# The norms' weight products move from the ternary layer into the channel attention; batch statistics one per slot

## What is computed

```python
x = x + tanh(g_xattn[0]) * L0_xattn(layernorm(x), ctx, mask, mask, ...)   # attention over channels, 16 heads of 8
x = x + tanh(g_ffn[0])   * L0_ffn(layernorm(x), ...)                      # ternary weights, 8-bit activations
x = x + tanh(g_xattn[1]) * L1_xattn(layernorm(x), ctx, ...)               # token attention, rms norm of q and k
x = x + tanh(g_ffn[1])   * L1_ffn(layernorm(x), ...)                      # attention and routed experts

q = rms_norm(x @ q_w + q_b, nq_s)     # in L1_xattn: the mean square goes over all 16 heads x 128
k = rms_norm(ctx @ ki_w + ki_b, nki_s)
```

## Time and profile before

| | |
|---|---|
| Three executions | 1869.86, 1876.90, 1881.18 us; median 1876.9 us |
| The profiled execution | span 1872.4 us, 34349 instructions |
| TensorE busy | 1729.6 us (92%) |
| VectorE busy | 1150.4 us (61%) |
| ScalarE busy | 976.9 us (52%) |
| GpSimd busy | 519.3 us (28%) |
| Mean granted clock of TensorE | 0.952 of 2.4 GHz |

### The profile page before, as it was taken

The page is one execution under the profiler, slowest core; times in us unless marked ns, Lnnn a source line. Parts: engine busy times, 40 slices in busy tenths (PEclk is TensorE's granted clock), DMA queues, the critical chain, the costliest instruction groups (busy, mean ns, idle before and its releaser), DMA issues. The chain is left out here.

```text
span 1872.4 us, 34349 instructions
## 1 busy us (share of the span) xinstructions
PE 1729.6 (92%) x11722; PEld 1454.1 (78%) x11722; DVE 1150.4 (61%) x2612; ACT 976.9 (52%) x2534; POOL 519.3 (28%) x570
## 2 busy tenths in 40 slices
PE   7999996897699999999999999999999988698887
PEld 6666663655588888888888888888888886587775
DVE  6689983897655656556566655555555658633334
ACT  2588875586354545545555545454454437344442
POOL 4133321253411111111122111121111221656663
PEclk7799996998899999999999999999999989899998
DMA  4111121202100100100100021001000024423346
GB/s 151 59 36 36 37 82 35 109 9 94 49 13 1 46 12 12 35 12 12 35 24 23 12 61 35 12 12 35 1 12 1 1 74 123 136 78 112 97 132 223
DMA packets 48914, 97.38 MB, mean 52 GB/s; under 512 B 7466, under 2 KB 29146, under 8 KB 47764
## 3 DMA queue, kind: packets, MB, share of 16 engines
q1 hardware_dynamic: 40023, 72.44, 12.7%
q0 software_dynamic: 7584, 21.37, 3.8%
q10 hardware_dynamic: 1144, 1.40, 0.2%
HBM read 73.85 MB, written 20.97 MB: 51 GB/s over the span
## 5 line engine op out<-in xcount | busy, mean ns | idle before, releaser
L2050 POOL TENSOR_TENSOR hold_wq<-hold_wq,ca_rsum 128x512 f32<-128x512 f32 x128 | 133.5, 1043 | 811.0 <-DVE ca_rsum L2290 811.0
L1906 ACT ACTIVATE hold_wq<-hold_wq,ca_nb,ca_evens 128x128 f32<-128x128 f32 x256 | 123.4, 483 | 226.9 <-DVE ca_nb L2285 226.9
L1906 ACT ACTIVATE hold_wq<-hold_wq,ca_nb,c_rqs 128x128 f32<-128x128 f32 x256 | 123.4, 483 | 223.8 <-DVE ca_nb L2285 223.8
L712 DVE TENSOR_REDUCE a_mx<-a_s 128x2 f32<-128x512 f32 x256 | 164.9, 681 | 43.3 <-PE a_s L584 40.6
L503 ACT ACTIVATE a_prob<-a_s 128x512 f32<-128x512 f32 x256 | 146.7, 604 | 61.1 <-PE a_s L604 60.0
L2066 PE MATMUL ca_qk<-early_x,ca_wqkv_h 128*128 128x512 f32 x384 | 161.5, 421 | 11.3 <-DVE ca_wqkv_l L2235 11.3
L2068 PE MATMUL ca_qk<-early_x,ca_wqkv_l 128*128 128x512 f32 x384 | 152.3, 397 | 0.0
L2067 PE MATMUL ca_qk<-early_x,ca_wqkv_h 128*128 128x512 f32 x384 | 151.6, 395 | 0.0
L2187 PE MATMUL ca_acc<-ca_wo_h,ca_oT_h 128*128 128x256 f32 x512 | 145.1, 283 | 0.2 <-DVE ca_oT_l L2299 0.2
L2189 PE MATMUL ca_acc<-ca_wo_h,ca_oT_l 128*128 128x256 f32 x512 | 144.4, 282 | 0.0
L2188 PE MATMUL ca_acc<-ca_wo_l,ca_oT_h 128*128 128x256 f32 x512 | 144.4, 282 | 0.0
(11 more groups left out here) (496 smaller groups left out, 4903.8 us busy)
## 6 DMA issues: line engine op xcount, KB each, us to landing
early_big<-slot_results SPq DMA_DIRECT2D x16, 512.0 KB, 4.7
mw_raw<-in_d_expert_w SPq DMA_DIRECT2D x12, 352.0 KB, 5.6
a_heads<-a_osb SPq DMA_DIRECT2D x124, 32.0 KB
a_wraw<-a_heads SPq DMA_DIRECT2D x31, 128.0 KB, 2.1
mw_down<-in_d_expert_d SPq DMA_DIRECT2D x1, 2816.0 KB
token_rows<-early_rows SPq DMA_DIRECT2D x1, 2176.0 KB
hold_wk<-in_c_wkT SPq DMA_DIRECT2D x1, 2064.0 KB
hold_wq<-in_c_wqT SPq DMA_DIRECT2D x1, 2064.0 KB
```

Source lines behind the costliest of these rows:

```text
L712: dve.tensor_reduce(mx[:, b % 2, :, h], s1_bank(b, u)[:, :, :], AX.X, ALU.max)\
L1906: ins = act.activation(prob[:, p, b, :], prob[:, p, b, :], ACT.Exp, bias=nb[:, p, b:b + 1], scale=row_scale[layer][:, r:r + 1], accum_out= ...
L2050: pool.tensor_tensor(prob[:, k % 2, :, :], prob[:, k % 2, :, :], rsum[:, k % 2, :].unsqueeze(2).broadcast_to([P, GB, TOKENS]), ALU.mult)\
```

## The change

`KeyWork` gets the three steps of a product (`multiply` for one head, `keep_high`, `keep_low`), and the channel attention runs them: product 0 in slots 0 to 10 and product 1 in slots 13 to 23, one or two heads a slot, both in the bank `out`; product 2 in slots 239 to 254, one head a slot, in `proj[0]`; product 3 behind the last slot, in a score bank. The evictions stand in the slot behind each product, the last ones at the end of ScalarE's and VectorE's queues. TensorE waits for a lower half before it writes the bank again. The ternary layer loses all of this. The fetch of the key weights goes ahead of the three transfers of 1536 KB, that of the query weights from behind batch 11 to behind batch 10. The measures of batches 4 to 15 go from threes in the slots below 0 to one a slot in slots 4 to 15, `condense` to slot 17, the power to 21, the bias to 26.

```diff
+    def multiply(self, pe, i, h, bank):
+
+        n, k = divmod(i, KT)
+        if h == 0:
+            pe.wait_ge(self.ld_w[n], 16)
+        mm = pe.matmul(bank[:, 0:GW], self.weights[n][:, h, P * k:P * k + P], self.weights[n][:, h, :],
+                       start=(h == 0), stop=(h == HEADS - 1))
+        if h == HEADS - 1:
+            mm.then_inc(self.gram_psum, 1)
+
+    def keep_high(self, act, i, bank):
+        act.wait_ge(self.gram_psum, i + 1)
+        act.activation(self.high(i // KT, i % KT), bank[:, 0:GW], ACT.Copy).then_inc(self.gram_hi, 1)
+
+    def keep_low(self, dve, i, bank):
+        dve.wait_ge(self.gram_hi, i + 1)
+        dve.tensor_tensor(self.low(i // KT, i % KT), bank[:, 0:GW], self.high(i // KT, i % KT).bitcast(F32),
+                          ALU.subtract).then_inc(self.gram_lo, 1)
...
 
+        gram_bank = [b[:, :, :].rearrange("p a n -> p (a n)") for b in (out, out, proj[0], s1[0])]
+
...
-        REST_POW, REST_BIAS = 12, 20
+        MEASURED, CONDENSED = 4, 17
+        REST_POW, REST_BIAS = 21, 26
+        GRAM_FROM, GRAM_SLOTS = (0, 13, 239), (11, 11, 16)
+
+        def gram_of(t):
+
+            for i, (a, n) in enumerate(zip(GRAM_FROM, GRAM_SLOTS)):
+                if 0 <= t - a < n:
+                    return i, range(HEADS * (t - a) // n, HEADS * (t - a + 1) // n)
+            return 0, range(0)
+
+        def gram_made(t):
+
+            return {a + n: i for i, (a, n) in enumerate(zip(GRAM_FROM, GRAM_SLOTS))}.get(t)
         ORDER = ("q0", "q1", "k0", "k1", "v0")
...
                                  mparts[BATCHES * k:BATCHES * k + BATCHES, :].bitcast(F32)).then_inc(m_ext, 16)
+                work.fetch(sp, 0)
                 sp.dma_start(x_sb[:, rest, :], io["x"][rest].rearrange("b p n -> p b n")).then_inc(ld_x[1], 16)
                 sp.dma_start(ctx_sb[:, rest, :], io["ctx"][rest].rearrange("b p n -> p b n")).then_inc(ld_c[1], 16)
...
                 maxima(1)
-                work.fetch(sp, 0)
                 for b in range(BATCHES):
                     gather(b)
                     if b + 2 < BATCHES:
                         maxima(b + 2)
-                    if b == 11:
+                    if b == 10:
                         sp.wait_ge(cm_ready, BATCHES)
                         work.fetch(sp, 1)
...
                         if copied(t)[1] == 0:
                             gated_mask(copied(t)[0])
                         copy_out(*copied(t))
+                    if gram_made(t) is not None:
+                        work.keep_high(act, gram_made(t), gram_bank[gram_made(t)])
...
                 act.wait_ge(x_done, 3 * (BATCHES - 2))
                 act.dma_start(den[:, p, :], heads[p, 1]).then_inc(moved[p], 16)
+                work.keep_high(act, 3, gram_bank[3])
...
                     o = out_bank(b, j // 2)
                     if j == 0:
                         pe.wait_ge(v_ready, b + 1)
+                    if b == 0 and j == 0:
+                        pe.wait_ge(work.gram_lo, 2)
+                    if j % 2 == 0 and o is proj[0]:
+                        pe.wait_ge(work.gram_lo, 3)
                     if j % 2 == 0 and o is not out:
                         pe.wait_ge(k_stack, 2 * BATCHES)
                         pe.wait_ge(v_ready, BATCHES)
...
+
+                def gram_room(i):
+                    if i == 1:
+                        pe.wait_ge(work.gram_lo, 1)
+                    if i == 2:
+                        pe.wait_ge(k_stack, 2 * BATCHES)
+                    if i == 3:
+                        pe.wait_ge(prob_ready, ALL)
...
                             project(b, *PIECES[u], 1)
                         if u == 13:
                             project_v(b)
+                    i, turns = gram_of(t)
+                    for h in turns:
+                        if h == 0:
+                            gram_room(i)
+                        work.multiply(pe, i, h, gram_bank[i])
+                gram_room(3)
+                for h in range(HEADS):
+                    work.multiply(pe, 3, h, gram_bank[3])
...
                     u, b = t % U, built(t)
                     if b is not None and u in (2, 6, 10, 14):
                         stack_piece(b, *PIECES[u - 2])
-                    if t < 0 and u % 4 == 2:
-                        n = FIRST + 3 * (u // 4)
-                        dve.wait_ge(ld_x[1], 16)
-                        measure(n, n + 3)
-                    if t == 0:
+                    if FIRST <= t - MEASURED + FIRST < BATCHES:
+                        n = t - MEASURED + FIRST
+                        if n == FIRST:
+                            dve.wait_ge(ld_x[1], 16)
+                        measure(n, n + 1)
+                    if t == CONDENSED:
                         condense(FIRST, BATCHES, 2 * FIRST)
                     if t == REST_BIAS:
                         mean_bias(FIRST, BATCHES, 1)
...
                         invert(closed(t), 1)
                         if closed(t) == BATCHES - 1:
                             close_last()
+                    if gram_made(t) is not None:
+                        work.keep_low(dve, gram_made(t), gram_bank[gram_made(t)])
+                work.keep_low(dve, 3, gram_bank[3])
...
@@ -860,7 +920,6 @@
-                sp.wait_ge(gram_psum, 4)
...
                 turned_scale(0)
-                gram_high(0)
                 scaled_weights(0)
...
                     if n == 0:
                         pe.wait_ge(weights_ready, w + 1)
-                        if w == 1:
-                            pe.wait_ge(gram_lo, 3)
...
                 def turn_h(n):
                     after(pe, hT_ready, n)
-                    if n == 0:
-                        pe.wait_ge(gram_lo, 4)
...
-                gram(0, 0)
-                gram(0, 1)
                 weight_sum(0)
-                gram(1, 0)
                 turn_scale(0)
                 weight_sum(1)
...
-                    if n == -1:
-                        gram(3, 0)
...
-                        gram(1, 1)
-                        gram(2, 0)
-                        gram(2, 1)
                     if n == -1:
                         turn_scale(1)
-                        gram(3, 1)
...
                     for n in range(a, b):
-                        if n == 10:
-                            gram_low(2)
...
                     if n == -1:
                         clip_weights(2)
-                        gram_low(3)
```

28 lines of the change are left out of this document (1 added, 27 removed).

## The result

The changed kernel took 1882.11 us (median of 20 runs, 1877.47 to 1885.54), the kernel before 1874.44 us beside it (20 runs): a ratio of **1.0034** [1.0024, 1.0043], or 6 to 8 us slower. Beside other kernels on another chip it was 1.0033 [1.0020, 1.0046]. I had forecast 2 us faster. The size is within the half per cent that I had called hard to tell, but twenty runs tell it, and it has the other sign. The profiled execution has a span of 1882.1 us.

A forecast was written before the change was run, and what follows sets the result against it. Opening bound by VectorE, then half-clock TensorE; closing also lost clock; ternary prologue waited on VectorE's chain, then ScalarE. Opening +0.4, closing -1.3, end +0.45, ternary -1.5 made -2.0 us: 1875 us from median 1876.9, range 1864 to 1883.

The forecast's parts named there:

- Opening, slots 0 to 23: Channel attention's opening: TensorE's added heads and lone score slots at 0.43 us make slot 24 8.4 us later.
- The first rival: Opening and closing: a lone score slot costs 0.22 us, not 0.43; 1865 us in all, chance 0.17.
- Opening, slots 24 to 34: Behind both opening products: TensorE without gaps keeps clock 1.00, 7.6 us less; whole opening +0.4 us.
- the second rival: Clock falls in slots 24 to 30, VectorE bounding, and in the last batch: opening +7, 1888 us, chance 0.10.
- Measures and fetch: Opening: one-per-slot measures and early weight fetch cost 0; measures gone from before slot 0 give 0.4 us less.
- Closing: Slots 239 to 254 and behind: slot 258 1.1 us later, ScalarE and last weighing faster at full clock; -1.3 us.
- End: Behind the last slot: product 3 hidden under the closing chain, its low half behind VectorE's last addition; +0.45 us.
- Ternary layer: Its prologue: without products and evictions the scale rows come 1.9 us earlier, low clock gives 0.4 back; -1.5 us.
- Sum: Whole kernel: opening, closing, end and ternary terms together -2.0 us, giving 1875 us.

The follow-up runs named there:

- e11: Changed kernel with products 0 and 1 in groups of two or three heads, mostly in even slots 0 to 26 and slot 27; ratio 0.9984 to the kernel before.
- e8: The changed kernel run again with no edit; ratio 1.0033 to the kernel before.
- e13: Kernel before with only the measures, condensing and early weight fetch moved, all products left in the ternary layer; ratio 1.0013.
- e17: Kernel before with the measures moved as in the change, products and weight fetch as before; ratio 1.0012.
- e2: Kernel before with only products 2 and 3 moved to the channel attention, single heads in slots 239 to 254; ratio 1.0020.
- after: The changed kernel in its first profile; 1882.11 us, ratio 1.0034 to the kernel before.
- e7: Changed kernel plus 64 unneeded multiplies in the ternary layer where the products stood before, without evictions; ratio 1.0034 to the kernel before.
- e10: Changed kernel with product 1 in slots 17 to 27 instead of 13 to 23; ratio 1.0040 to the kernel before.
- e4: Changed kernel with products 0 and 1 in groups of five and six heads, product 2 in pairs in even slots; ratio 1.0024 to the kernel before.
- e15: Changed kernel with products 0 and 1 in groups of two and three, product 2 in pairs, product 3 back in the ternary layer; ratio 0.9978 to the kernel before.
- e12: Changed kernel with products 0 and 1 in groups of two and three heads and product 2 in pairs in even slots; ratio 0.9968 to the kernel before.
- e5: Kernel before with only products 2 and 3 moved, product 2 as two heads in each even slot 240 to 254; ratio 1.0013.
- e3: Kernel before with only product 3 moved, behind the last slot of the channel attention; ratio 1.0006.
- e6: Changed kernel plus six unneeded multiplies, two in each of slots 256 to 258; ratio 1.0040 to the kernel before.
- e9: The kernel before run again with no edit; ratio 0.9994.

## Why the prediction was wrong, point by point

**Opening, slots 0 to 23: right.** I had 8.4 us more at slot 24 from 21 lone slots at 0.43; measured 8.1 and 7.7. The first rival (a lone slot is cheap) is out. The rule that I had weighed from the Trainium skill (TensorEngine Tiling (Array Packing), "Key Properties": a change of tiling mode drains the engine) agrees with it: with half the changes (e11) some 5 us of the 8.1 vanish.

**Opening, slots 24 to 34: the step that failed.** I had 7.6 us back, since TensorE would have no gap and the clock 1.00: 10.3 us from slot 24 to slot 34's piece. They took 11.6 in the first profile and 14.5 to 15.5 in the four others. TensorE was full at 1.00 from 28 to 64 us, but then came two waits for ScalarE's first exponentials, 1.08 us together, which I had not looked for: I checked VectorE as the second bound there, in the second rival, and not the first exponentials. Slot 34 was at +1.8 in the first profile and +3.8 to +4.7 in the four others with this opening, slot 238 at +0.7 and +2.9 to +4.1. Term: +0.4 forecast, some **+3** measured. The second rival had the mechanism, but with +7 us and a clock that does not come back; it was back after 7 to 10 us. That rival was to turn on TensorE's share in these slots, which I had at 90%; it was 2.92 of 4 us, in the profile that kept the clock as in e8, which lost it.

**Measures and fetch: 0 and -0.4 us forecast.** Slot 0 came 0.1 to 1.2 us earlier, right. The 2 us that e13 and e17 measured I did not have; where they arise is open (above).

**Closing: -1.3 forecast.** Three sizes were off. A slot without a weighing took 1.06 us and a fourth of the slots, with one, 2.06: 1.31 us a slot on average where I had 1.2 (the head costs 0.63 and not 0.47 when it stands alone), and slot 258 came 3.5 us later than slot 238's piece would have it, not 1.1. From slot 242's turned maxima to slot 255's scores the rows above give 0.32 + 4 x 1.0 (weighings) + 13 x 0.63 + 12 x 0.43 = 17.7 us; I had 15.6, with thirteen quarters of a weighing where four whole ones stand and no turned maxima. The last three slots took 2.4 us and not 1.7, with 0.98 of waiting for exponentials. And the clock fell at 302 us, behind the last head, so that ScalarE's gain of 2.3 us came in full, of the kernels with lone heads, only in e2 (2.6 us from slot 258 to the last weighing; e8 1.3, after 0.2). From slot 238 to the last addition, kernels with lone heads took 0.7 to 3.4 us more than before (after 2.9, e8 1.8, e2 0.7, e7 3.4, e10 3.1, e11 2.4), with pairs -2.1 to +1.0 (e4, e15, e12, e5), and with no product there -3.9 to +1.5. Lone heads cost some **+2.5**, pairs about nothing; device times say the same of the step from one to the other (e11, e12).

**End: +0.45 forecast, +0.1 measured.** Product 3 took 7.25 us (319.35 to 326.6) under the closing chain, as forecast. Its low half stands behind the last addition, but from that addition to the next layer's first instruction were 1.85 us instead of 1.73: the meeting of all engines covers it. e3 measures 1.0006 [0.9989, 1.0023].

**Ternary layer: -1.5 forecast.** The seven kernels that take all products out of it (after, e4, e6, e8, e10, e11, e12) took -1.1 to +0.1 us from its first instruction to its last addition against the first profile of before, -0.7 in the mean; the second profile of before took +1.3. The saving is about 1 us and comes with products 0 and 1: the second scale rows begin 41.3 to 42.7 us after the layer's first instruction in the seven profiles without added work that keep these two there (before, e2, e3, e5, e9, e13, e17) and 39.9 to 40.9 in the twelve that don't, wherever products 2 and 3 stand. The 1.1 us that I had for the last product's own place is not there (e3, which moves this product alone: 41.8). The scale rows came 40.7 us after the layer's first instruction, not 38 as the prediction wrote nor the 39.7 of its own sum (41.6 before).

**Sum.** Some +3, +2.5, 0 and -1 are 4.5 us, and in profiles the changed kernel was 3.8 and 3.9 us behind at the ternary layer's end. Device time says 6 to 8. The rest, 2 to 3 us, arises in unchanged code behind it, 2.3 of it before the fourth layer in both profiles; the first profile with its 5.9 us overstates it.

**What I should have seen.** The prediction priced 21 changes there and back at 0.43 - 0.11 us and more, 9 us in all, and took them as given. The same sum with three heads in every second slot was there to be made from the earlier trace rows, and it is the version that wins.
